# The first node stage of a two-layer graph kernel, rearranged

## The chip, the cores and the metric

One core of one Trainium2 chip runs the whole kernel. The metric is the device time of one launch in microseconds (us).

## The reference

There are 6250 nodes and 200000 edges, both with 128 features; the edges are sorted by target. Two layers follow each other, each as x = x + layer(relu(layernorm(x))).

```python
# layer 0, message passing
h = relu(layernorm(x))
msg = relu(concat([h[src], h[dst], edge_attr]) @ msg_W1 + msg_b1) @ msg_W2 + msg_b2
agg = segment_sum(msg, dst)
u   = relu(concat([h, agg]) @ upd_W1 + upd_b1) @ upd_W2 + upd_b2
x   = x + layer_norm(h + u, gamma, beta)
# layer 1, attention with 4 heads of 32, self loops added
h = relu(layernorm(x))
x_l, x_r = h @ W_l.T + b_l, h @ W_r.T + b_r
e = einsum(leaky_relu(x_l[src] + x_r[dst], 0.2), att)
alpha = segment_softmax(e, dst)
x   = x + elu(segment_sum(alpha * x_l[src], dst) + bias)
```

## The kernel before

Nodes are worked on in tiles of 128 (49 tiles, `NT`), edges in groups of 512 (391 groups, `J` = 4 edges per partition). A group's targets all lie in a window of 32 nodes (`W`) whose first row is `base[g]`, so target rows are read as a window and source rows are gathered.

The program has three parts. The first node stage (`prelude`, L347 and on) normalises all nodes, multiplies them by the first third of `msg_W1` and stores the product as the table `tab_a`; it also turns the edge indices into the layout that the edges need, checks that the windows hold (`flag_i`) and stores the first `LEAD` = 5 tiles of the target table `tab_b3` in three bf16 parts. Then comes the MLP edge stage, which also does all node work between the layers, and then the attention edge stage. If the check fails, a general path runs in place of both (`is_fast`, `If`/`Else` in every engine).

In each edge stage GpSimd issues four indirect gathers per group (L858), of 128 rows each, into a ring of eight slots. Its first gather comes after the last store of `tab_a` (`k.a_stored`), the stores of the zero rows at the tables' ends (`s_tops`) and the flag have arrived. SyncE loads the edge features, target rows and windows.

The first node stage goes in chunks of `CH` = 4 tiles, thirteen of them, the last with one tile. Each engine runs its own list of steps n in program order, tied to the others by semaphores:

- SyncE (`first_sync`) loads the nodes X in seven pieces cut at `XCUT`, the source and target rows (`row_loads`), 18 weights and biases, then stores one chunk of `tab_a` after the other (L471), with the remaining small loads and the eleven zero rows `tops` (L466) in between, and the permuted target rows `dst_rows` (L469).
- VectorE computes statistics of chunk n (L694, L697), and of chunk n-1 the reciprocal (L726) and the negative scaled mean `nm` (L727). In some steps it also makes constants (L701 to L712), copies turned index rows (`take_rows`, L683), prepares attention weights (L715 to L722), makes `base` and the window ids (L748 to L751) and counts edges inside their window (L753 to L760) and ordered bases (L762 to L774).
- ScalarE does the square root of chunk n (L517), the relu copy of turned chunk n-2 into `HT` (L521), the scaling of three tiles of chunk n-1 (L529), and copies the product of chunk n-3 to the store's buffer (L536), of which there are two, so it waits for the store of two chunks before.
- GpSimd scales the fourth tile (L580), casts both index tables to float (L588, L591) and permutes the target rows (L593).
- TensorE turns chunk n-1 (L627), multiplies chunk n-2 (L635), and in some steps turns index rows (L609) and spreads the bases over the partitions (L657).

After the stage SyncE loads the first eight groups' edges (`load_edges`), stores the early target tiles (`store_early`, L480), waits for both stores and loads the eight windows (`load_targets`).

Of the kernel before, what the change touches and what calls it, by code (L numbers as in the profile page):

```python
# [14 lines left out]
BF16 = mybir.dt.bfloat16  # L15
# [15 lines left out]
LEAD = 5  # L31
TINY = 1e-16
# [66 lines left out]
def gnn_program(nc, t):  # L99
# [22 lines left out]
    assert k.groups % U == U - 1 and CH < LEAD <= 2 * CH and NR - 1 <= NT  # L122
# [224 lines left out]
def prelude(nc, t, k, ctx, sems, ring, xn, at, r1, spare, stats):  # L347
# [7 lines left out]
    assert 2 * NBLK <= U and G * J <= 4 * EG  # L355
    s, s_x, s_ast, s_bst = k.first

    def sb(name, shape, dt=F32):
# [4 lines left out]
    rel = ring[:, 0:U].rearrange("p u j d -> p (u j d)")[:, 0:G * J].rearrange("p (g j) -> p g j", j=J)  # L363
    hit = ring[:, 0:U].rearrange("p u j d -> p (u j d)")[:, 4 * EG:4 * EG + G * J]
    perm = sb("perm", [GB, NBLK, EG], I16)
    cnt = sb("cnt", [P, 4])
    warm = sb("warm", [P, 1])
# [5 lines left out]
    b3 = [spare[:, 0:6 * P].bitcast(BF16).rearrange("p (t c d) -> p t c d", t=CH, c=3),  # L373
          spare[:, 6 * P:6 * P + (LEAD - CH) * 3 * P // 2].bitcast(BF16).rearrange("p (t c d) -> p t c d", c=3, d=P)]
# [63 lines left out]
    def first_sync(sp):  # L438
        sp.wait_ge(s["s_zt"], 1)
        for n, (a, b) in enumerate(zip(cuts, cuts[1:])):  # L440
            if n == 2:
                sp.wait_ge(s["s_pool"], 2)
                row_loads(sp, 0, "src", s["s_src"])
# [5 lines left out]
        if len(cuts) < 4:  # L449
            sp.wait_ge(s["s_pool"], 2)  # L450
            row_loads(sp, 0, "src", s["s_src"])
        row_loads(sp, 1, "dst", s["s_dst"])
        sp.wait_ge(s["s_pool"], 3)
        z16 = k.zrow[:].bitcast(BF16)[:, 0:P]
        top = k.NP - W
        tops = [(tab[top:k.NP, part, :], z16) for tab in (k.tab_b3, k.tab_r3) for part in range(3)]
        tops += [(tab[top:k.NP, :], k.zrow[:]) for tab in (k.tab_b, k.tab_r, k.tab_a, k.tab_l)]
        tops.append((k.tab_es[:, top:k.NP], k.zrow[0:H, 0:W]))
        for dst, src in weights[:8]:
            sp.dma_start(dst, src).then_inc(s["s_wt"], 16)  # L460
        for c in range(NC):
            for dst, src in weights[8 + 5 * (c - 1):8 + 5 * c if c < NC - 1 else None] if c else []:
                sp.dma_start(dst, src).then_inc(s["s_wt"], 16)
            if c == min(5, NC - 1):
                for dst, src in tops:
                    sp.dma_start(dst, src).then_inc(s["s_tops"], 16)  # L466
            if c == min(9, NC - 1):
                sp.wait_ge(s["s_conv"], 3)
                sp.dma_start(k.dst_rows.rearrange("(b g) e -> g b e", g=GB), perm[:]).then_inc(s["s_permout"], 16)  # L469
            sp.wait_ge(s["a_a"], c + 1)  # L470
            sp.dma_start(k.tab_a[c * CH * P:(c * CH + size(c)) * P, :].rearrange("(t p) d -> p t d", p=P),  # L471
                         at[c % 2][:, 0:size(c), :]).then_inc(s_ast[c % 2], 16)
        sp.wait_ge(s["s_permout"], 16)
# [3 lines left out]
    def store_early(sp):  # L477
        for c in range(2):
            sp.wait_ge(s["a_lo"], c + 1)
            sp.dma_start(k.tab_b3[c * CH * P:(c * CH + early(c)) * P, :, :].rearrange("(t p) c d -> p t c d", p=P),  # L480
                         b3[c][:, 0:early(c)]).then_inc(s_bst[c], 16)
        for one in s_bst:
            sp.wait_ge(one, 16)
# [26 lines left out]
    def first_scalar(act):  # L510
# [3 lines left out]
        for n in range(NC + 3):  # L514
# [8 lines left out]
            if 0 <= n - 1 < NC:  # L523
# [3 lines left out]
                for q in range(min(size(c), CH - 1)):  # L527
# [13 lines left out]
        for c in range(2):  # L541
# [6 lines left out]
    def first_gpsimd(pool):  # L548
# [26 lines left out]
        def scale(c):  # L575
            if size(c) == CH:
                i = c * CH + CH - 1
                pool.wait_ge(s["a_nm"], c + 1)
                after(pool, s["a_tp"], c - 1)
                pool.tensor_scalar(xn[c % 2][:, CH - 1, :], k.X[:, i, :], rs[:, i:i + 1], nm[:, i:i + 1], ALU.mult,  # L580
                                   ALU.add).then_inc(s["a_xp"], 1)

        for c in range(max(NC, NBLK + 4)):
            if c < NC:
                scale(c)
            if c == 0:
                pool.wait_ge(s["s_src"], n_rows)
                pool.tensor_copy(rows_f[:, 0], rows_i[:, 0]).then_inc(s["s_conv"], 1)  # L588
            if c == 3:
                pool.wait_ge(s["s_dst"], n_rows)  # L590
                pool.tensor_copy(rows_f[:, 1], rows_i[:, 1]).then_inc(s["s_conv"], 1)  # L591
            if 0 <= c - 4 < NBLK:
                last = pool.tensor_copy(perm[:, c - 4, :].rearrange("g (j p) -> g j p", j=J),  # L593
                                        rows_i[:, 1, c - 4, :].rearrange("g (p j) -> g j p", j=J))
                if c - 4 == NBLK - 1:
                    last.then_inc(s["s_conv"], 1)
# [5 lines left out]
    def first_tensor(pe):  # L602
# [10 lines left out]
        for n in range(steps):  # L613
            if n == 2:
                pe.wait_ge(s["s_w1"], 16)
            if n == 9:
# [27 lines left out]
            if n == 6:  # L644
                for b in range(min(2, NBLK)):
                    turn_rows(NBLK + b)
            if n == 7:
                for b in range(2, NBLK):
                    turn_rows(NBLK + b)
            if n == 11:  # L650
# [4 lines left out]
            if n == 9:  # L655
# [5 lines left out]
        pe.wait_ge(s["a_a"], NC)  # L661
        for c in range(2):
            for q in range(early(c)):
                i = c * CH + q
                last = pe.matmul(p_ab[c][:, q * P:(q + 1) * P], lhsT=k.HT[:, i * P:(i + 1) * P],
# [5 lines left out]
    def first_vector(dve):  # L671
# [18 lines left out]
        for n in range(steps):  # L690
# [8 lines left out]
            if n == 1:  # L699
# [13 lines left out]
            if n == 10:  # L713
# [9 lines left out]
            if 0 <= n - 1 < NC:  # L723
                c = n - 1
                dve.wait_ge(s["a_sd"], c + 1)
                link(dve.reciprocal(rs[:, tiles(c)], sd[:, tiles(c)]))  # L726
                dve.scalar_tensor_tensor(out=nm[:, tiles(c)], in0=mv[:, tiles(c), 0], scalar=-1.0, in1=rs[:, tiles(c)],  # L727
                                         op0=ALU.mult, op1=ALU.mult).then_inc(s["a_nm"], 1)
            if n == 4:
                for b in range(min(2, NBLK)):  # L730
                    take_rows(b)
            if n == 5:
                for b in range(2, NBLK):
                    take_rows(b)
            if n == 7:
                for b in range(min(2, NBLK)):
                    take_rows(NBLK + b)
            if n == 8:
                for b in range(2, NBLK):
                    take_rows(NBLK + b)  # L740
            if n == 13:
# [3 lines left out]
            if n == 10:  # L745
                dve.wait_ge(s["s_conv"], 3)
# [5 lines left out]
            if n == 11:  # L752
                link(dve.tensor_tensor(rel, k.dst_t[:, 0:G, :],  # L753
                                       k.base[:].unsqueeze(2).to_broadcast([P, G, J]), ALU.subtract))
            if n == 11:
                hits = hit.rearrange("p (g j) -> p g j", j=J)
# [21 lines left out]
        for c in range(2):  # L778
            dve.wait_ge(s["a_bp"], c + 1)
            dve.tensor_tensor(bt[c][:, 0:early(c), :],  # L780
                              p_ab[c][:, 0:early(c) * P].rearrange("p (t d) -> p t d", d=P),
                              k.b1_bc[:].unsqueeze(1).to_broadcast([P, early(c), P]), ALU.add).then_inc(s["a_b"], 1)
        for c in range(2):
# [3 lines left out]
        for c in range(2):  # L787
# [7 lines left out]
    return first_sync, store_early, first_scalar, first_gpsimd, first_tensor, first_vector  # L795
# [1608 lines left out]
```

## Time and profile before

| | us |
|---|---|
| median of 3 runs | 4030.74 (4029.25 to 4032.33) |
| the profiled execution | 4030.37 |
| its span, first to last instruction | 4028.5 |
| TensorE busy | 2958.8 (73%) |
| VectorE busy | 1939.5 (48%) |
| ScalarE busy | 1763.4 (44%) |
| GpSimd busy | 2986.6 (74%) |
| mean granted TensorE clock | 0.809 |

Busy time is a share of the whole span. GpSimd's busy time is nearly all gathers; the short time in which it issues each of them isn't counted as busy. A releaser that a view names is inferred from the semaphores.

### The profile page before, as it was taken

The page shows a single profiled execution, that of the slowest core. Times are in us where ns is not written, and L with a number is a line of the kernel's source. Part 1 is how long each engine was busy: PE and PEld are TensorE (multiplying, and loading weights), DVE is VectorE, ACT ScalarE, POOL GpSimd, SP SyncE. Part 2 cuts the span into 40 slices and gives each one's busy share as a digit, 9 for nine tenths or more (in the row PEclk, how much of TensorE's full clock was granted, in tenths as well). Part 3 has the DMA queues.
Part 4 walks back from the last instruction along what each step waited for, and adds up shares of the span by engine and source line. Part 5 has one row for each costly group of instructions (what it writes and reads, how often), then busy time and mean ns, then how long its engine had stood idle before and what let it go on. Part 6 is the DMA issues. An engine that isn't in the chain of part 4 may idle for free.

```text
span 4028.5 us, 83733 instructions
## 1 busy us (share of the span) xinstructions
PE 2958.8 (73%) x29662; PEld 2146.4 (53%) x29662; DVE 1939.5 (48%) x7746; ACT 1763.4 (44%) x4374; POOL 2986.6 (74%) x3167
## 2 busy tenths in 40 slices
PE   5877777778787787777867777766777766766776
PEld 4666666666666666666634444444444444444443
DVE  5334343444343434343435555555555555555555
ACT  4233333333333333333335555555555555555555
POOL 5777777777777777777757777777777777777775
PEclk8787787877787878787768888888888888888888
DMA  6444444444444444444423333333333333333332
GB/s 179 133 136 137 136 139 136 137 137 136 136 137 136 137 136 137 136 139 133 118 76 86 86 89 86 88 86 87 87 86 87 86 87 86 87 86 87 87 87 61
DMA packets 335748, 447.91 MB, mean 111 GB/s; under 512 B 150181, under 2 KB 190595, under 8 KB 335327
## 3 DMA queue, kind: packets, MB, share of 16 engines
q1 hardware_dynamic: 234831, 237.29, 19.9%
q0 software_dynamic: 100096, 205.00, 18.8%
q8 instruction: 241, 3.95, 0.4%
q14 instruction: 180, 1.47, 0.1%
q10 hardware_dynamic: 400, 0.20, 0.0%
HBM read 422.12 MB, written 20.07 MB: 110 GB/s over the span
## 4 chain that ended last, share of the span: by engine, by line
POOL 43%; PE 19%; DMA 17%; issue 17%; DVE 3%; ACT 2%; SPq 1%; DVEq 0%; POOLq 0%; ACTq 0%
POOL m_ring L858 27%; POOL t_ring L858 16%; DMA t_ring<-tab_l,src_t 13%; PE bank L2202 3%; DMA m_ring<-tab_a,src_t 3%; PE bank L2196 3%; PE bank L1473 3%; PE bank L2193 2%; PE bank L1465 1%; PE bank L2211 1%; PE bank L2214 1%; DVE m_pre L1560 1%; PE bank L2186 1%; PE bank L1475 1%; PE bank L1483 1%
## 5 line engine op out<-in xcount | busy, mean ns | idle before, releaser
L858 POOL DMA_INDIRECT t_ring<-tab_l,src_t x1564 | 1481.9, 948 | 500.7 <-issue 366.7
L858 POOL DMA_INDIRECT m_ring<-tab_a,src_t x1564 | 1484.9, 949 | 485.4 <-issue 468.3
L1560 DVE TENSOR_TENSOR m_pre<-bank,m_ring 128x512 f32<-128x512 f32 x391 | 270.3, 691 | 1109.5 <-DMA m_ring<-tab_a,src_t 813.9
L1521 ACT ACTIVATE m_hid<-m_pre 128x512 f32<-128x512 f32 x391 | 246.5, 631 | 1131.8 <-DVE m_pre L1560 1120.8
L1473 PE MATMUL bank<-w,m_attr_t 128*128 128x128 f32 x3128 | 703.1, 352 | 15.3 <-ACT m_attr_t L1517 15.3
L1473 PEld LDWEIGHTS bank<-w,m_attr_t 128*128 128x128 f32 x3128 | 608.7, 242 | 59.4 <-DVE m_hot L1551 23.8
L2193 PE MATMUL bank<-t_hot_t,t_win 96*128 96x512 bf16 x391 | 166.3, 425 | 571.0 <-DMA t_ring<-tab_l,src_t 498.8
L2242 ACT ACTIVATE t_z<-bank 128x512 f32<-128x512 f32 x391 | 233.4, 597 | 706.3 <-PE bank L2196 703.5
L2202 PE MATMUL bank<-t_zt,att_wn 128*128 128x512 f32 x782 | 537.8, 778 | 0.0
L2341 DVE TENSOR_TENSOR t_old<-acc,t_shrink 128x64 f32<-128x64 f32 x391 | 90.4, 231 | 804.1 <-ACT t_shrink L2253 674.9
L1475 PE MATMUL bank<-m_win,m_hot_t 96*128 96x128 bf16 x1564 | 393.5, 252 | 0.0
L2193 PEld LDWEIGHTS bank<-t_hot_t,t_win 96*128 96x128 bf16 x391 | 38.5, 98 | 657.7 <-issue 491.9
L2211 PEld LDWEIGHTS bank<-t_a_edge,t_ring 128*32 128x32 f32 x12512 | 157.9, 125 | 414.7 <-issue 406.1
L1483 PE MATMUL bank<-m_hid,m_hot 128*32 128x129 f32 x3128 | 188.7, 318 | 244.7 <-ACT m_hid L1521 243.9
L1465 PE MATMUL bank<-ident,m_ring 128*128 128x128 f32 x1564 | 303.9, 329 | 18.3 <-DMA m_win<-tab_b 18.3
L2237 ACT ACTIVATE t_a_edge<-bank 128x512 f32<-128x512 f32 x391 | 232.6, 595 | 193.3 <-PE bank L2186 188.0
L2196 PE MATMUL bank<-ident,t_ring 128*128 128x128 f32 x1564 | 286.2, 314 | 0.0
L1517 ACT ACTIVATE m_attr_t<-bank 128x512 f32<-128x512 f32 x391 | 229.8, 588 | 128.3 <-PE bank L1465 127.9
L2247 ACT ACTIVATE t_a_row<-t_logit,t_den_max 128x512 f32<-128x512 f32 x391 | 278.7, 713 | 0.5 <-DVE t_den_max L2309 0.5
L2256 ACT ACTIVATE t_pen<-t_hot_t,t_big 128x512 f32<-128x512 bf16 x391 | 277.5, 710 | 0.0
L2303 DVE TENSOR_TENSOR t_zt<-bank,t_z 128x512 f32<-128x512 f32 x391 | 264.0, 675 | 10.3 <-ACT t_z L2242 10.3
L2309 DVE CUSTOM_DVE_ANT_0 t_logit<-bank,t_pen 128x512 f32<-128x512 f32 x391 | 265.5, 679 | 1.1 <-PE bank L2202 1.0
(252 smaller groups left out, 5163.4 us busy)
## 6 DMA issues: line engine op xcount, KB each, us to landing
m_ring<-in_edge_attr_dram SPq DMA_DIRECT2D x390, 256.0 KB
t_rows<-dst_rows SPq DMA_DIRECT2D x196, 256.0 KB
m_rows<-dst_rows SPq DMA_DIRECT2D x196, 192.0 KB
m_ring<-tab_a,src_t POOLq DMA_INDIRECT x1564
t_ring<-tab_l,src_t POOLq DMA_INDIRECT x1564
m_win<-tab_b SPq DMA_DIRECT2D x391, 24.0 KB
t_win<-tab_r SPq DMA_DIRECT2D x391, 24.0 KB
tab_b<-n_b SPq DMA_DIRECT2D x47, 96.0 KB
```

The source lines that it names most:

```text
L858: pool.indirect_dma_start(out=r.got[u][0:rows, j, :], out_offset=None, in_=table, in_offset=bass.IndirectOffsetOnAxis(ap=k.src_t[0:rows, g ...
L1465: last = pe.transpose(p_attr[u % 2][:, j * P:(j + 1) * P], attr[u][:, j, :], k.ident[:])
L1473: pe.matmul(p_hid[q % 2][:, e], lhsT=attr_t[q % 2][:, e], rhs=k.w1[:, 2, :], start=True, stop=False)
L1475: last = pe.matmul(p_hid[q % 2][:, e], lhsT=hot_t[q % 2][0:3 * W, e], rhs=r.win[q][:], start=False, stop=True)
L1560: dve.tensor_tensor(pre[q % 2][:], p_hid[q % 2][:], r.got[q][:].rearrange("p j d -> p (j d)"), ALU.add).then_inc(s["m_sum"], 1)
L2193: pe.matmul(p_z[q % 2][:], lhsT=r.win[q][:], rhs=hot_t[q % 2][0:3 * W, :], start=True, stop=False)
L2196: last = pe.matmul(p_z[q % 2][:, j * P:(j + 1) * P], lhsT=r.got[q][:, j, :], rhs=k.ident[:], is_transpose=True, start=False, stop=(j == J ...
L2202: pe.matmul(p_e[q % 2][:], lhsT=k.att_wn[:], rhs=zt[q % 2][:], start=True, stop=True).then_inc(s["t_ep"], 1)
L2247: act.activation(a_row[q % 2][:], logit[q % 2][:], ACT.Exp, scale=-1.0, bias=den_max[q % 4][:, 1:2], accum_out=den_max[q % 4][:, 0:1]).the ...
L2256: act.activation(pen[q % 4][:], hot_t[q % 2][:], ACT.Identity, bias=big[:, 0:1], scale=-BIG).then_inc(s["t_pen"], 1)
L2303: dve.tensor_tensor(zt[q % 2][:], p_z[q % 2][:], z02[q % 2][:], ALU.max).then_inc(s["t_z"], 1)
L2309: dve.tensor_tensor_reduce(out=logit[q % 2][:], in0=p_e[q % 2][:], in1=pen[q % 4][:], scale=1.0, scalar=3.0e38, op0=ALU.add, op1=ALU.min, ...
```

## The change

All of it lies in the first node stage and in SyncE's first round after it.

- GpSimd scales two of a chunk's four tiles (`SCALED` = 2), ScalarE two.
- The check that every edge lies in its group's window is made on the index rows, which have 98 partitions with 4 x 512 entries (a group each): GpSimd clips each row to its window (`clip_rows`), and one VectorE pass counts the entries that clipping left as they were. The four passes over the turned layout of 1568 entries go.
- SyncE loads four pieces of nodes before the source and target rows, the rest after them, the last piece after the first table store. The 18 small loads and 11 zero rows are issued three at a time ahead of each table store. The permuted rows are stored after the twelfth chunk's store (before: before the tenth's).
- The casts, the turning of index rows, the base and the weight work come one to three steps later; VectorE's `reciprocal` and `nm` come ahead of the steps' extra work.
- The early target tiles are made and stored as two and three tiles (before: four and one), each finished before the next is begun; the first window is loaded between the two stores, and the edge loads of later groups come between the windows.

```diff
+SCALED = 2
+FRONT = 2
...
+    ends = sb("row_ends", [GB, 2, NBLK])
+    clipped = k.acc[0:GB, 0, P:P + NBLK * EG].rearrange("p (b e) -> p b e", b=NBLK)
...
     def early(c):
-        return min(CH, LEAD - c * CH)
+        return (LEAD - FRONT) if c else FRONT
...
     def first_sync(sp):
...
+        for n in range(min(4, many)):
+            load_nodes(n)
+        sp.wait_ge(s["s_pool"], 2)
+        row_loads(sp, 0, "src", s["s_src"])
+        row_loads(sp, 1, "dst", s["s_dst"])
+        for n in range(4, many - 1):
+            load_nodes(n)
+        store_sources(0)
+        if many > 4:
+            load_nodes(many - 1)
+        sp.wait_ge(s["s_pool"], 3)
+        small = [(dst, src, s["s_wt"]) for dst, src in weights] + [(dst, src, s["s_tops"]) for dst, src in tops]
+        per = -(-len(small) // max(min(10, NC - 2), 1))
+        for c in range(1, NC):
+            for dst, src, done in small[per * (c - 1):per * c if c < NC - 1 else None]:
+                sp.dma_start(dst, src).then_inc(done, 16)
+            store_sources(c)
+            if c == NC - 2:
+                sp.wait_ge(s["s_conv"], 3)
+                sp.dma_start(k.dst_rows.rearrange("(b g) e -> g b e", g=GB), perm[:]).then_inc(s["s_permout"], 16)
...
     def first_scalar(act):
-                for q in range(min(size(c), CH - 1)):
+                for q in range(CH - SCALED if size(c) == CH else size(c)):
...
     def first_gpsimd(pool):
+                for q in range(CH - SCALED, CH):
+                    i = c * CH + q
+                    last = pool.tensor_scalar(xn[c % 2][:, q, :], k.X[:, i, :], rs[:, i:i + 1], nm[:, i:i + 1],
+                                              ALU.mult, ALU.add)
+                last.then_inc(s["a_xp"], 1)
+        def clip_rows():
+            pool.tensor_scalar(ends[:, 0, :], rows_f[:, 1, :, 0], float(k.NP - W), 0.0, ALU.min, ALU.max
+                               ).then_inc(s["s_pool"], 1)
+            pool.wait_ge(s["s_pool"], 6)
+            pool.tensor_scalar(ends[:, 1, :], ends[:, 0, :], float(W - 1), None, ALU.add).then_inc(s["s_pool"], 1)
+            pool.wait_ge(s["s_pool"], 7)
+            for b in range(NBLK):
+                last = pool.tensor_scalar(clipped[:, b, :], rows_f[:, 1, b, :], ends[:, 0, b:b + 1],
+                                          ends[:, 1, b:b + 1], ALU.max, ALU.min)
+            last.then_inc(s["s_pool"], 1)
-            if c == 0:
+            if c == 2:     # cast of the source rows
-            if c == 3:
+            if c == 4:     # cast of the target rows
+            if c == 5:
+                pool.wait_ge(s["s_conv"], 2)
+                clip_rows()
-            if 0 <= c - 4 < NBLK:
+            if 0 <= c - 7 < NBLK:     # permutation
...
     def first_tensor(pe):
-            if n == 3:                # turn_rows: 3, 4, 6, 7
+            if n == 5:                # 5, 6, 7, 8
-            if n == 9:                # weights turned, base spread
+            if n == 11:               # weights turned
+            if n == 10:               # base spread
-        pe.wait_ge(s["a_a"], NC)
         for c in range(2):
+            pe.wait_ge(s["a_a"], NC - 1 + c)
...
     def first_vector(dve):
-            if n == 1:                # constants, ahead of reciprocal and nm
+            if n == 3:                # constants, behind them
-            if n == 10:               # weights, ahead of reciprocal and nm
+            if n == 12:               # weights, behind them
-            if n == 4:                # take_rows: 4, 5, 7, 8
+            if n == 7:                # 7, 8, 9, 10
-            if n == 10:               # base, window ids
+            if n == 11:
-            if n == 11:
-                link(dve.tensor_tensor(rel, k.dst_t[:, 0:G, :],
-                                       k.base[:].unsqueeze(2).to_broadcast([P, G, J]), ALU.subtract))
-                link(dve.tensor_scalar(hits, rel, 0.0, None, ALU.is_ge))
             if n == 12:
-                link(dve.scalar_tensor_tensor(out=rel, in0=rel, scalar=float(W), in1=hits, op0=ALU.is_lt, op1=ALU.mult))
-                link(dve.tensor_reduce(cnt[:, 0:1], rel, mybir.AxisListType.XY, ALU.add))
+                link(dve.memset(cnt[:], 0.0))
+                dve.wait_ge(s["s_pool"], 8)
+                link(dve.scalar_tensor_tensor(out=clipped, in0=clipped, scalar=0.0, in1=rows_f[:, 1], op0=ALU.add,
+                                              op1=ALU.is_equal, accum_out=cnt[0:GB, 0:1]))
...
         def fast_sync(sp):
-                    for u in slots:
+                    for u in range(2):
                         load_edges(sp, u, u)
-                    store_early(sp)
-                    for u in slots:
+                    store_early(sp, 0)
+                    early_stored(sp, 0)
+                    load_targets(sp, 0, 0)
+                    store_early(sp, 1)
+                    load_edges(sp, 2, 2)
+                    early_stored(sp, 1)
+                    for u in range(1, U):
                         load_targets(sp, u, u)
+                        if u + 2 < U:
+                            load_edges(sp, u + 2, u + 2)
```

The remarks behind `#` are put in here; they name the code that moves, unchanged, and its steps before and after.

## Rows read from the trace of the kernel before

**Rows 1.** The page's groups: line, engine, operation, count, busy us, mean ns, idle before.

```profile
L858 POOL DMA_INDIRECT m_ring<-tab_a,src_t x1564 | 1484.9, 949 | 485.4 <-issue 468.3
```

**Rows 2.** GpSimd's waits, whole span: total us, times, longest us.

```profile
POOL m_ring L858 <- issue: 468.3, 1508, 8.9
...
POOL t_ring L858 <- DMA tab_l<-m_attr_t: 24.3, 1, 24.3
...
POOL m_ring L858 <- PE bank L1475: 11.6, 38, 0.3
```

**Rows 3.** Timeline of GpSimd: start us, length us, what, idle before it.

```profile
60.62 1.26 POOL L858 DMA_INDIRECT m_ring<-tab_a,src_t  x1 [8.86 <-issue]
...
2021.16 0.90 POOL L858 DMA_INDIRECT m_ring<-tab_a,src_t  x1 [0.30 <-issue]
2046.37 0.95 POOL L858 DMA_INDIRECT t_ring<-tab_l,src_t  x1 [24.31 <-DMA tab_l<-m_attr_t]
```

**Rows 4.** Timeline of all engines, first 30 us.

```profile
6.81 0.15 DVE L701 TENSOR_SCALAR thirds<-thirds 128x42 f32<-128x42 f32 x1
...
9.24 1.26 ACT L529 ACTIVATE m_attr_t<-X,nm,rs 128x128 f32<-128x128 f32 x3 [2.02 <-DVE nm L727]
...
11.47 0.87 DVE L694 BATCH_NORM_STATS2 m_hid<-X 128x6 f32<-128x128 f32 x4 [2.26 <-DMA X<-in_x_dram]
...
17.65 0.60 ACT L536 ACTIVATE m_pre<-bank 128x512 f32<-128x512 f32 x1
...
23.32 1.89 POOL L591 CAST m_ring<-m_ring 98x2048 f32<-98x2048 int32 x1 [6.79 <-DMA m_ring<-in_dst_dram]
23.34 1.89 DVE L727 SCALAR_TENSOR_TENSOR nm<-mv,rs 128x4 f32<-128x4 f32 x1
...
27.73 0.45 POOL L580 TENSOR_SCALAR m_attr_t<-X,rs,nm 128x128 f32<-128x128 f32 x1 [0.91 <-DVE nm L727]
```

**Rows 5.** Timeline of all engines, 30 to 78 us.

```profile
31.04 0.60 ACT L536 ACTIVATE m_pre<-bank 128x512 f32<-128x512 f32 x1 [1.70 <-DMA tab_a<-m_pre]
...
37.82 0.30 ACT L517 ACTIVATE sd<-mv,eps 128x4 f32<-128x4 f32 x1 [1.13 <-DVE mv L697]
...
40.13 0.29 ACT L517 ACTIVATE sd<-mv,eps 128x4 f32<-128x4 f32 x1
...
43.02 0.57 DVE L748 TENSOR_SCALAR base<-bank 128x392 f32<-128x392 f32 x1 [2.07 <-PE bank L657]
...
53.50 0.16 DVE L727 SCALAR_TENSOR_TENSOR nm<-mv,rs 128x1 f32<-128x1 f32 x1
...
57.06 0.28 ACT L536 ACTIVATE m_pre<-bank 128x128 f32<-128x128 f32 x1 [0.95 <-DMA tab_a<-m_pre]
...
77.04 1.97 PE L1465 MATMUL bank<-ident,m_ring 128*128 128x128 f32 x8 [18.27 <-DMA m_win<-tab_b]
```

**Rows 6.** Groups by shape, GpSimd and VectorE, first stage.

```profile
L593 POOL CAST perm<-m_ring 98x512 int16<-98x512 int32 x4 | 4.4, 1104 | 0.0
...
L760 DVE TENSOR_REDUCE cnt<-m_ring 128x1 f32<-128x1568 f32 x1 | 1.8, 1786 | 0.0
L759 DVE SCALAR_TENSOR_TENSOR m_ring<-m_ring 128x1568 f32<-128x1568 f32 x1 | 1.8, 1785 | 0.0
L753 DVE TENSOR_TENSOR m_ring<-dst_t,base 128x1568 f32<-128x1568 f32 x1 | 1.8, 1782 | 0.0
L757 DVE TENSOR_SCALAR m_ring<-m_ring 128x1568 f32<-128x1568 f32 x1 | 1.1, 1116 | 0.0
```

**Rows 7.** Chain of waits in order of time: start us, us, what.

```profile
24.32 6.63 DMA tab_a<-m_pre
...
54.69 2.28 DMA tab_a<-m_pre
```

**Rows 8.** Stretches of 2 us: busy per engine, TensorE clock, DMA share, GB/s.

```profile
10.00:12.00 2.00, 1.09 (x4) 0.71 (x4) 0.53 (x3) 0.51 (x2) 1.84 (x1) 1.00 1.20 290
...
18.00:20.00 2.00, 2.00 (x11) 2.00 (x11) 0.00 (x0) 1.54 (x5) 0.00 (x0) 1.00 1.02 233
```

More of the change, by code:

```diff
@@ L121, in gnn_program @@
     k.ahead = min(k.NT - 1, NR)
-    assert k.groups % U == U - 1 and CH < LEAD <= 2 * CH and NR - 1 <= NT
+    assert k.groups % U == U - 1 and FRONT < LEAD <= FRONT + CH and LEAD * 3 <= 16 and NR - 1 <= NT
     assert k.tiles >= NR - 4 and NR > 4
@@ L354, in prelude @@
     cuts = [c for c in XCUT if c < NT] + [NT]
-    assert 2 * NBLK <= U and G * J <= 4 * EG
+    assert 2 * NBLK <= U and G <= EG
     s, s_x, s_ast, s_bst = k.first
@@ L438, in first_sync, with load_nodes @@
     def first_sync(sp):
[L439 to L443, printed above, removed]
+        top = k.NP - W
+        z16 = k.zrow[:].bitcast(BF16)[:, 0:P]
+        tops = [(tab[top:k.NP, part, :], z16) for tab in (k.tab_b3, k.tab_r3) for part in range(3)]
+        tops += [(tab[top:k.NP, :], k.zrow[:]) for tab in (k.tab_b, k.tab_r, k.tab_a, k.tab_l)]
+        tops.append((k.tab_es[:, top:k.NP], k.zrow[0:H, 0:W]))
+        def load_nodes(n):
+            a, b = cuts[n], cuts[n + 1]
             if min(b, nt) > a:
@@ L448, in first_sync, with store_sources @@
                 sp.dma_start(k.X[0:k.LAST, nt, :], t["x"][nt * P:k.N, :]).then_inc(s_x[n], 16)
[L449 to L469, printed above, removed]
+        def store_sources(c):
             sp.wait_ge(s["a_a"], c + 1)
@@ L472, in first_sync @@
                          at[c % 2][:, 0:size(c), :]).then_inc(s_ast[c % 2], 16)
+        sp.wait_ge(s["s_zt"], 1)
+        many = len(cuts) - 1
+        for n in range(min(4, many)):
[18 more added lines that the diff above has]
+                sp.dma_start(k.dst_rows.rearrange("(b g) e -> g b e", g=GB), perm[:]).then_inc(s["s_permout"], 16)
         sp.wait_ge(s["s_permout"], 16)
@@ L475, in first_sync, with store_early, early_stored @@
         sp.wait_ge(s["s_tcopy"], 2 * NBLK)
[L477 to L483, printed above, removed]
+    def store_early(sp, c):
+        sp.wait_ge(s["a_lo"], c + 1)
+        sp.dma_start(k.tab_b3[first(c) * P:(first(c) + early(c)) * P, :, :].rearrange("(t p) c d -> p t c d", p=P),
+                     b3[c][:, 0:early(c)]).then_inc(s_bst[c], 16)
+    def early_stored(sp, c):
+        sp.wait_ge(s_bst[c], 16)
     def general_rows_tensor(pe):
@@ L660, in first_tensor @@
         pe.matmul(p_misc[:, 0:1], lhsT=k.ones[:], rhs=cnt[:, 2:3], start=True, stop=True).then_inc(s["s_flagp"], 1)
-        pe.wait_ge(s["a_a"], NC)
         for c in range(2):
+            pe.wait_ge(s["a_a"], NC - 1 + c)
             for q in range(early(c)):
-                i = c * CH + q
-                last = pe.matmul(p_ab[c][:, q * P:(q + 1) * P], lhsT=k.HT[:, i * P:(i + 1) * P],
+                i = first(c) + q
+                last = pe.matmul(p_ab[(NC + c) % 2][:, q * P:(q + 1) * P], lhsT=k.HT[:, i * P:(i + 1) * P],
                                  rhs=k.w1[:, 1, :], start=True, stop=True)
@@ L780, in first_vector @@
             dve.tensor_tensor(bt[c][:, 0:early(c), :],
-                              p_ab[c][:, 0:early(c) * P].rearrange("p (t d) -> p t d", d=P),
+                              p_ab[(NC + c) % 2][:, 0:early(c) * P].rearrange("p (t d) -> p t d", d=P),
                               k.b1_bc[:].unsqueeze(1).to_broadcast([P, early(c), P]), ALU.add).then_inc(s["a_b"], 1)
-        for c in range(2):
             dve.wait_ge(s["a_hi"], c + 1)
```

61 lines of the change are left out of this document (26 added, 35 removed).

## The prediction

> **What bounds the kernel now.** I read the page first, then GpSimd's waits over the whole span, then its timeline at its two starts, then the timeline of the first 66 us with the chain of waits through it.
>
> The page's costliest groups are the gathers of L858: 1564 in each of the two edge stages, about 0.95 us each [rows 1]. GpSimd's waits show what is between them: 0.30 us of issue each time, longer only twice. Once is 8.9 us before the first gather, once 24.3 us between the stages, where it waits for the stored table tab_l. A row that names TensorE as releaser has no wait over 0.3 us [rows 2], so no other engine holds the stream up. The first gather starts at 60.62, the last of the MLP stage ends at 2022.06, the next stage starts at 2046.37 [rows 3]. That is 1961.4 us for 1564 gathers, 1.254 us each, with nothing in it that this change touches. So the change is worth what it moves the first gather, one for one: time = 4030.37 - (60.62 - new start). The profiled execution's own 4030.37 is its span of 4028.5 plus 1.9 around it; the median of the runs is 4030.74, so I add 0.4 at the end.
>
> The reader should then look at what ends last before 60.62. I number as the code does: chunk c is 4 node tiles (12 chunks, and a 13th of one tile), at(c) is ScalarE's copy of its table rows (L536), nm(c) VectorE's L727, step n ScalarE's turn that begins with the square root of chunk n. GpSimd waits for the last tab_a store, which follows at(12) at 57.06, which follows nm(12) at 53.50 [rows 5]. From nm(12) to the first gather are 7.1 us.
>
> **The change part by part.** I follow four checkpoints: at(0), at(3), the start of step 10, nm(12). Before they are 17.65, 31.04, 40.13 and 53.50 [rows 4, 5].
>
> *Start.* The constants (L701 to L712) stood between the square root and nm(0), from 6.81 until ScalarE's scaling at 9.24 could start; they now come two steps later, which frees 2.0 us. It isn't this that decides: statistics of chunk 2 waited for their node load until 11.47 [rows 4], and 0.8 MB of source rows were ahead of it in the queue. At some 0.27 MB/us (0.29 in one stretch of the loads, 0.23 in a later one [rows 8]) these are 2.9 us, so chunk 2 arrives at about 8.6. From there at(0) came 6.2 us later; two scalings in this stretch now have two tiles on ScalarE, not three. One tile is 1.26/3 = 0.42 us [rows 4], so at(0) lands at 8.6 + 6.2 - 0.8 = 14.0, 3.6 earlier.
>
> *Stretch to at(3): transfers.* at(3) waited 1.70 us for the store of chunk 1, which the chain shows under way for 6.63 us behind weight loads [rows 5, 7]. By rates alone, the computing would now be at at(3) around 23. But the queue has a floor: ahead of the landing of that store stand the first weight (0.19 MB), all nodes (3.2), both row tables (1.6), the store of chunk 0 (0.26), three weights (0.26) and the store itself (0.26), 5.8 MB in all, since the last node load is now put between the stores of chunks 0 and 1. From 2 us on at 0.29 for nodes and 0.245 for rows that is 23.0, and 1.3 us until the store counts (2.28 us for one alone [rows 7], less its 0.95 us of bytes). So at(3) is at 24.4, 6.6 earlier. At 0.25 throughout it would be 26.4; with no queue at all, 23. The wait for destination rows (GpSimd idle 6.79 us until 23.32 [rows 4]) goes, since they land near 16; VectorE's nm(4), which was caught for 1.89 us behind that cast, is freed with it.
>
> *GpSimd's load in the middle.* It gets a second scaling per chunk: 0.45 us alone [rows 4], so 12 x 0.45 = 5.4 us in all, beside ScalarE's 0.84 of the same chunk and ready earlier, since it needn't wait for ScalarE's relu copy. Cost nothing while GpSimd is not late. The range check adds two short instructions (0.3 each at most) and four of 98x512. No row has this operation at this size. Below: 0.45 + 384 x 0.92 ns (the slope of the 98x2048 cast, 1.89 us [rows 4]) = 0.8 us. Above: four times the 128-wide one, 1.8. I take 1.1, the 98x512 cast of L593 [rows 6]. Check: 5.0 us (3.8 to 7.8). It starts after the destination cast and the scaling of chunk 5, near 19.3, so chunk 6 is scaled by 25.2; ScalarE's own half of chunk 6 isn't done before 26.6 (24.4, its own 0.6, root and relu copy 0.8, two tiles 0.84), as it is held by the store. Cover 1.4 us: nothing at 1.1 each, 1.4 us at 1.8. The Trainium skill, GPSIMD Engine Reference, section 3.1, gives 1.8 cycles per element for such a loop, 0.77 us for 512 elements. By it the check would be 3.7 us and as hidden; the sum stays.
>
> *at(3) to step 10.* This took 9.1 us [rows 5]. Three scalings lose a tile each (-1.3). The turning of rows is moved, but both pairs of destination rows lie in this stretch before and after. SyncE now issues three small loads before each store instead of eleven table tops in a block: stores of chunks 3 to 5 have two or three broadcasts ahead of them. The 6.63 us store had five, and exceeded a lone one by 4.3, mostly bytes; I allow 1.0 for these (0 to 3). So 9.1 - 1.3 + 1.0 = 8.8, step 10 starts at 33.2.
>
> *Step 10 to nm(12).* The base matmul is moved one step, so is VectorE's wait for it. Base (L748) started 5.2 us after the start of step 9 [rows 5]; now it is one tile less after that of step 10: +4.8. From there nm(12) was 10.5 us away. Four passes of 1568 elements go: 1.79 + 1.78 + 1.78 + 1.12 = 6.5 [rows 6]. One pass over 2048 comes: 1.785 x 2048/1568 = 2.3 (2.0 to 3.0; its accumulator is not in any row). Statistics of chunk 11 now precede base (-1.3), the weight block (1.4) moves behind it. 10.5 - 6.5 + 2.3 - 1.3 + 1.4 = 6.4; with memset and links 6.6. nm(12) = 33.2 + 4.8 + 6.6 = 44.6, 8.9 earlier.
>
> *nm(12) to the gather.* 7.1 us as before, with the same wait of at(12) for the store of chunk 10. New is that the permuted rows (392 x 1 KB) are stored between the last two table stores, not three chunks earlier: 0.4 MB is 1.5 us in the same queue, partly beside at(12). I take 1.0 (0 to 1.5). The flag is ready earlier: nine short operations follow nm(12), as before. First gather: 44.6 + 7.1 + 1.0 = 52.7, a shift of 7.9.
>
> *Target rows.* Storing two tiles first brings group 0's window long before the 77 us at which TensorE began [rows 5]; its eight groups of lead belong to the ring, and GpSimd didn't wait for TensorE even so [rows 2]. Worth nothing, costs nothing: the new chain of alternate VectorE and ScalarE work is longer, yet TensorE still starts some 15 us earlier.
>
> Sum: 4030.37 - 7.9 + 0.4 = 4022.8.
>
> **The rivals.**
> 1. *Stalls between the checkpoints eat part of it* (shift 2 to 6, say 4026.8). For it: queue at 0.25 (+2), GpSimd's check at the upper end (+1.4), the broadcasts at 3 (+2). All are bounds named above. Against: each has some cover.
> 2. *The middle runs freely* (shift 10 to 13, say 4019.3): TensorE is kept busy from earlier on, transfers land at 0.29 throughout and no store is waited for. For it: ScalarE's own work is only about 1.9 us a chunk. Against: the queue floor.
> 3. *Slower: GpSimd becomes the bound of the first stage.* VectorE's nm(4) took 1.89 us because GpSimd was casting [rows 4]; its two-input operations wait for GpSimd's current one. So a slow check on GpSimd, at chunk 5, holds both nm(6) and the scaling of chunk 6. It decides from 1.45 us an instruction (cover gone), and eats the whole gain from 1.45 + 7.9/4 = 3.4 us each; at 5.6 us each the kernel is 8.8 us slower, 4039. Against: nearest rows end at 1.8. The Trainium skill, GPSIMD Engine Reference, section 8, says that it shares its SBUF interfaces with VectorE and contends with two-input instructions; the row agrees (1.89 instead of 0.16), and it advises VectorE for elementwise work.
> 4. *It doesn't do what it says*: the new count differs from the constant that the flag compares with, and the general path runs, many times slower. The sentinel in padded rows is clipped to another value, so padding isn't counted, as before.
>
> **How the numbers follow.** 0.2% of 4030.7 is 8.1 us, about what a measurement here can tell from no change; my shift of 7.9 lies on it. Forecast (shift 6 to 10) 0.58, rival 1 0.19, rival 2 0.19, rival 3 0.03, rival 4 0.01. Over 8.1: half of the forecast's and all of rival 2's, 0.48. Within: 0.48. Slower: 0.04. Range: from a shift of 3 to one of 13, 4017.7 to 4027.8.
>
> **What would show it.** First gather between 51 and 55, gathers still 0.30 apart, the gap between stages still about 24 us. at(0) near 14, at(3) near 24 with a wait for a store, step 10 near 33, nm(12) near 45 with one pass of about 2.3 us ahead of it. GpSimd's four check instructions near 1.1 each. TensorE's edge work starting near 60 with nothing gained from it. The prediction is wrong if the first gather isn't the shift, or if ScalarE waits for GpSimd's half of chunk 6.

## The result and the profile after

| | before | after |
|---|---|---|
| median, same chip, 6 runs each | 4031.26 (4028.79 to 4034.16) | 4051.11 (4047.47 to 4051.82) |
| the profiled execution, and its span | 4030.37, 4028.5 | 4051.45, 4049.6 |
| first gather starts | 60.62 | 58.72 |
| one gather, median of 1564 and 1564 | 944 and 944 ns | 952 and 952 ns |
| mean granted TensorE clock | 0.809 | 0.811 |

The ratio is 1.0048 (1.0035 to 1.0061, a 95% interval): slower by half a per cent, where I had forecast 4022.8. Two things differ from the forecast. The first gather came 1.9 us earlier, not 7.9. And each gather takes longer, in both edge stages. From the page of the changed kernel, the rows that answer to [rows 1] (busy us, mean ns of one):

```profile
L880 POOL DMA_INDIRECT t_ring<-tab_l,src_t x1564 | 1493.1, 955 | 500.6 <-issue 368.4
L880 POOL DMA_INDIRECT m_ring<-tab_a,src_t x1564 | 1496.9, 957 | 487.8 <-issue 472.6
```

Before, the second of them was

```profile
L858 POOL DMA_INDIRECT t_ring<-tab_l,src_t x1564 | 1481.9, 948 | 500.7 <-issue 366.7
```

From 1484.9 and 1481.9 the busy time rose to 1496.9 and 1493.1, together 23.2 us. Less the 1.9 us of the earlier start that is 21.3; the spans differ by 21.1. Nothing else is left to explain. GpSimd's waits show that it isn't idleness, the answer to [rows 2] (us in total, times, longest):

```profile
POOL m_ring L880 <- issue: 472.6, 1514, 11.4
POOL t_ring L880 <- PE bank L2224: 56.7, 186, 0.3
POOL t_ring L880 <- DMA tab_l<-m_attr_t: 24.3, 1, 24.3
```

Still 0.3 us between gathers and 24.3 between the stages. So the instruction itself is slower. One view of the line of the gathers gives the median (min/median/max ns, first and last start); before and after:

```profile
L858 POOL DMA_INDIRECT m_ring<-tab_a,src_t x1564: 892/944/1257, 60.6 to 2021.2; - x196
L858 POOL DMA_INDIRECT t_ring<-tab_l,src_t x1564: 896/944/1083, 2046.4 to 4003.8; - x196
L880 POOL DMA_INDIRECT m_ring<-tab_a,src_t x1564: 896/952/1347, 58.7 to 2031.1; - x196
L880 POOL DMA_INDIRECT t_ring<-tab_l,src_t x1564: 897/952/1092, 2056.3 to 4024.9; - x196
```

The change doesn't touch these instructions: in both traces GpSimd issues the same 3128 gathers, in the same order, with the same shapes.

The first stage, from the timeline (start, length, line, operation, idle time before and what ended it), in place of [rows 4, 5]:

```profile
14.08 0.60 ACT L550 ACTIVATE m_pre<-bank 128x512 f32<-128x512 f32 x1 [0.34 <-PE bank L664]
14.50 1.89 POOL L614 CAST m_ring<-m_ring 98x2048 f32<-98x2048 int32 x1 [2.32 <-DMA m_ring<-in_src_dram]
14.63 1.77 DVE L732 SCALAR_TENSOR_TENSOR nm<-mv,rs 128x4 f32<-128x4 f32 x1
22.38 8.25 POOL L605 TENSOR_SCALAR acc<-m_ring,row_ends 98x512 f32<-98x512 f32 x4
24.84 0.60 ACT L550 ACTIVATE m_pre<-bank 128x512 f32<-128x512 f32 x1 [1.48 <-DMA tab_a<-m_pre]
25.86 0.16 DVE L732 SCALAR_TENSOR_TENSOR nm<-mv,rs 128x4 f32<-128x4 f32 x1
30.62 1.72 POOL L594 TENSOR_SCALAR m_attr_t<-X,rs,nm 128x128 f32<-128x128 f32 x4
31.59 1.08 PE L656 MATMUL bank<-ident,m_attr_t 128*128 128x128 f32 x4 [5.68 <-issue]
32.71 0.60 ACT L535 ACTIVATE HT<-bank 128x512 f32<-128x512 f32 x1 [5.17 <-PE bank L656]
38.34 0.29 ACT L531 ACTIVATE sd<-mv,eps 128x4 f32<-128x4 f32 x1
43.77 0.56 DVE L776 TENSOR_SCALAR base<-bank 128x392 f32<-128x392 f32 x1 [2.97 <-PE bank L686]
47.59 2.29 DVE L783 SCALAR_TENSOR_TENSOR acc<-acc,m_ring 98x2048 f32<-98x2048 f32 x1
50.12 0.16 DVE L732 SCALAR_TENSOR_TENSOR nm<-mv,rs 128x1 f32<-128x1 f32 x1
58.72 1.35 POOL L880 DMA_INDIRECT m_ring<-tab_a,src_t  x1 [11.43 <-issue]
```

| checkpoint | predicted | after | difference that arose since the last checkpoint |
|---|---|---|---|
| at(0) | 14.0 | 14.08 | +0.1 |
| at(3) | 24.4 | 24.84 | +0.4 |
| start of step 10 | 33.2 | 38.34 | +4.7, most of it the clipping on GpSimd (e8) |
| nm(12) | 44.6 | 50.12 | +0.4 |
| first gather | 52.7 | 58.72 | +0.5 |

The four clipping instructions (max with one end, min with the other) take 8.25 us, 2.06 each. They are in front of GpSimd's half of chunk 6 (30.62); TensorE stands still for 5.68 us until it can turn that chunk, and ScalarE's relu copy waits 5.17 us. VectorE isn't held by them: in the middle of the clipping `nm` takes 0.16 us (25.86). It was held by a cast on GpSimd, once more: nm(3) takes 1.77 us (14.63) beside the cast of the source rows (14.50).

TensorE's first work of the edge stage starts at 67.87, where it was 77.04; I had said near 60. The gathers don't wait for it.

### The profile page after: what moved, and what is told of

It is laid out like the page before. It is cut to its first block, busy times and chain, and to the rows that moved or that the text cites. A ratio compares the mean times of both kernels' runs of the same rounds, so it can differ in the third digit from the quotient of the medians.

```text
span 4049.6 us, 83736 instructions
## 1 busy us (share of the span) xinstructions
PE 2949.8 (73%) x29662; PEld 2139.6 (53%) x29662; DVE 1934.3 (48%) x7745; ACT 1759.2 (43%) x4362; POOL 3020.9 (75%) x3185
## 4 chain that ended last, share of the span: by engine, by line
POOL 45%; issue 18%; DMA 17%; PE 17%; DVE 2%; ACT 2%; SPq 0%; DVEq 0%; POOLq 0%; ACTq 0%
POOL m_ring L880 28%; POOL t_ring L880 17%; DMA t_ring<-tab_l,src_t 13%; DMA m_ring<-tab_a,src_t 3%; PE bank L2224 3%; PE bank L2230 3%; PE bank L1501 3%; PE bank L2221 2%; PE bank L1493 1%; DVE m_pre L1588 1%; PE bank L2239 1%; PE bank L2242 1%; PE bank L1503 1%; PE bank L1511 1%; PE bank L1518 0%
## 5 line engine op out<-in xcount | busy, mean ns | idle before, releaser
L880 POOL DMA_INDIRECT t_ring<-tab_l,src_t x1564 | 1493.1, 955 | 500.6 <-issue 368.4
L880 POOL DMA_INDIRECT m_ring<-tab_a,src_t x1564 | 1496.9, 957 | 487.8 <-issue 472.6
L2214 PE MATMUL bank<-ident,t_a_row 128*128 128x128 f32 x1564 | 267.8, 299 | 1.1 <-ACT t_a_row L2275 1.1
```

The source lines that it names most:

```text
L880: pool.indirect_dma_start(out=r.got[u][0:rows, j, :], out_offset=None, in_=table, in_offset=bass.IndirectOffsetOnAxis(ap=k.src_t[0:rows, g ...
L2214: last = pe.transpose(p_turn[:, e], a_row[q % 2][:, e], k.ident[:])
```

## The experiments

One theory is needed for each of the two losses. For the late first gather: *the clipping on GpSimd is slow and ScalarE and TensorE wait behind it.* For the slower gathers, where the trace shows no cause, the candidates were: I, that max/min ran on GpSimd at all; II, that GpSimd scales two tiles; III, the memory and the layout of the changed stage; IV, GpSimd's instruction count ahead of the gathers, or which instruction is last; V, the order of its clipping and its permutation of target rows (the last permutation is a cast to int16 at chunk 10, before at chunk 7). The recorded expectations name theories by letters of their own, each explained where it first comes.

The first four kernels and the last two (e13, e15) ran at a lower granted clock (0.70 to 0.72), where the kernel before takes 4933.56 and 4970.75 us and gathers do wait for other engines. Their totals (e1 4929.27, e2 4939.88, e3 4938.34, e4 4914.42, e13 4968.83, one execution each) can't be compared with the other ones, and so don't test the times that were expected of them. A gather's length can be compared: 944 ns (e1, e2) and 952 ns (e4, e13, e15) both come at this clock, as both come at 0.81.

**e1: clipping on VectorE at step 12.** The two short and four long instructions are moved from GpSimd to VectorE, otherwise after.

```diff
-            if c == 5:
-                pool.wait_ge(s["s_conv"], 2)
-                clip_rows()
...
             if n == 12:
+                for b in range(NBLK):
+                    last = dve.tensor_scalar(clipped[:, b, :], rows_f[:, 1, b, :], ends[:, 0, b:b + 1],
+                                             ends[:, 1, b:b + 1], ALU.max, ALU.min)
```

> The changed kernel, with the six clipping operations moved from GpSimd to VectorE (step 12). The traces of before and after show two things: the first gather starts at 58.7 instead of 60.6, and each of the 3128 gathers takes 952 instead of 944 ns (medians), 3128 x 7.5 ns = 23.5 us. Theory A (an operation of new kind on GpSimd, the clipping by max and min, leaves each later gather 8 ns slower): the gathers are back at 944 here. Theory B (the number of GpSimd's instructions or their place in the program sets it): 944 or 952, no link with clipping. In both, the stall in the middle (TensorE waited 5.7 us for chunk 6) goes, and VectorE gets about 2 us more: first gather at 53 to 56. So the time is about 4024 to 4026 by A, and 4047 by B if the gathers stay slow.

Measured: gathers 944 and 944 ns, first gather 57.00 (53 to 56 expected). The slower gathers hang on the clipping being on GpSimd; candidates II and III fall, since this kernel has both.

```profile
L871 POOL DMA_INDIRECT m_ring<-tab_a,src_t x1564: 894/944/1152, 57.0 to 2447.5; - x196
```

**e2: before, and clipping on GpSimd at chunk 9.** Its result is unused. In the kernel before, chunk 9 is behind the last permutation.

> The kernel before, with the same six clipping operations added on GpSimd behind its permutation; their result is used by nothing. Theory A: gathers at 952 ns, 4030 + 24 = 4054 plus a few us of stall. Theory B: gathers at 944 if nothing else moves them, time 4031 to 4036.

Measured: 944 and 944 ns, first gather 64.57. The same six instructions on the same engine, and no effect: candidate I falls as it stands, and with e1 the place of these six instructions is what is left to test.

**e3 and e4: the scaling alone.** e3 is before with two tiles scaled by GpSimd; e4 is after with `SCALED = 1`.

> The kernel before, with two tiles of a chunk scaled by GpSimd instead of one, nothing else changed. Theory A: gathers stay at 944 ns; the first gather starts 1 to 4 us earlier, 4027 to 4030. Theory B (number of GpSimd's instructions): 12 more instructions may move the gathers to 952, then about 4052.

> The changed kernel with one tile of a chunk scaled by GpSimd, as before, and the clipping left on it. Theory A: gathers stay at 952 ns, time 4050 to 4056. Theory B: 12 instructions fewer, gathers may be back at 944, then 4028 to 4032.

Measured: e3 947 and 946 ns, first gather 60.48, 0.1 us earlier than before and not 1 to 4; e4 952 and 952 ns, 58.60. Two scaled tiles aren't the cause of the 8 ns. The 2 to 3 ns of e3 stay unexplained.

**e5 and e6: the same clipping, late in after and early in before.** In e5 it comes at chunk 9 of after, still ahead of the last permutation; in e6 at chunk 5 of before, ahead of the last permutation too.

```diff
-            if c == 5:
+            if c == 9:
                 pool.wait_ge(s["s_conv"], 2)
                 clip_rows()
```

> The changed kernel with GpSimd's six clipping operations moved from its chunk 5 to its chunk 9. What is known: the gathers' instructions are the same in all kernels, yet their median is 944 ns in the kernel before, 952 in the changed one, 944 with the clipping off GpSimd, 944 with it added late to the kernel before, 952 in the changed kernel with one tile scaled, 946 to 947 with two tiles scaled in the kernel before. Theory C (the order of GpSimd's operations ahead of the gathers sets the gathers' time; clipping early gives 952): 944 here. Theory D (something of the changed kernel other than the place of clipping, together with clipping): 952. Either way TensorE's wait for chunk 6 goes, another for chunk 10 comes; first gather at 57 to 61.

> The kernel before with the six clipping operations added on GpSimd at its chunk 5, result unused. Theory C: gathers at 952 ns. Theory D: 944, as when they were added at chunk 9.

Measured: e5 952 and 952 ns, first gather 58.11, 4048.57 us; e6 952 and 952 ns, 67.95, 4062.15 us, where before took 4031.16. Nothing of the change but the clipping is in e6, and the gathers are slow:

```profile
L875 POOL DMA_INDIRECT m_ring<-tab_a,src_t x1564: 896/952/1196, 67.9 to 2041.7; - x196
```

and of e2, the same instructions behind the last permutation:

```profile
L875 POOL DMA_INDIRECT m_ring<-tab_a,src_t x1564: 896/944/1196, 64.6 to 2455.6; - x196
```

**e7: one memset as GpSimd's last operation.** After, and `pool.memset(ends[:, 0, 0:1], 0.0)` ahead of its waits for the stores.

> The changed kernel with one more GpSimd instruction, a memset of one column, as its last before it waits for the table stores. Theory E (the number of GpSimd's instructions ahead of the gathers, that is their place in its program, sets the time): another median than 952. Theories C and D: 952. First gather at 58.7 as in the changed kernel.

Measured: 952 and 952 ns, first gather 58.48, 4050.75 us. Candidate IV falls for this instruction: neither one more nor another last one helps. e2 and e6 have equally many instructions ahead of the gathers, and differ by 8 ns.

**e8: the whole row check in VectorE's gap.** Clipping and count go to VectorE at step 11, ahead of its wait for the bases, where it is idle; nothing of them is left on GpSimd.

```diff
             if n == 11:
+                for b in range(NBLK):
+                    last = dve.tensor_scalar(clipped[:, b, :], rows_f[:, 1, b, :], ends[:, 0, b:b + 1],
+                                             ends[:, 1, b:b + 1], ALU.max, ALU.min)
+                link(last)
+                link(dve.memset(cnt[:], 0.0))
+                link(dve.scalar_tensor_tensor(out=clipped, in0=clipped, scalar=0.0, in1=rows_f[:, 1], op0=ALU.add,
+                                              op1=ALU.is_equal, accum_out=cnt[0:GB, 0:1]))
                 dve.wait_ge(s["s_basep"], 1)
```

> The changed kernel with the clipping on VectorE and, with the counting pass, put ahead of VectorE's wait for the bases (step 11), where the trace of after has it idle for 2.97 us. Six clipping operations of 98x512 at most are about 2 us and the count 2.3 us. The stall of 5.2 us on GpSimd's half of chunk 6 goes and 2.3 us of counting leave the end: first gather at 52 to 55 instead of 58.7. With gathers at 944 ns (clipping not on GpSimd, as in the first such run) the time is 4022 to 4025 where before has 4031; with 952 it is 4046 to 4049.

Measured: 4025.18 us (4022.39 to 4026.87) against 4031.16, ratio 0.9983 (0.9974 to 0.9993). It is 0.2% faster than before, and 26 us under the 4051.11 of the changed kernel, though the two weren't timed side by side. From its timeline, and the view of its gathers:

```profile
33.71 0.29 ACT L531 ACTIVATE sd<-mv,eps 128x4 f32<-128x4 f32 x1
34.74 2.73 DVE L764 TENSOR_SCALAR acc<-m_ring,row_ends 98x512 f32<-98x512 f32 x4
37.63 2.29 DVE L768 SCALAR_TENSOR_TENSOR acc<-acc,m_ring 98x2048 f32<-98x2048 f32 x1
39.96 0.57 DVE L771 TENSOR_SCALAR base<-bank 128x392 f32<-128x392 f32 x1
43.83 0.16 DVE L718 SCALAR_TENSOR_TENSOR nm<-mv,rs 128x1 f32<-128x1 f32 x1
53.22 1.15 POOL L870 DMA_INDIRECT m_ring<-tab_a,src_t  x1 [9.74 <-issue]
```

```profile
L870 POOL DMA_INDIRECT m_ring<-tab_a,src_t x1564: 898/944/1152, 53.2 to 2014.1; - x196
L870 POOL DMA_INDIRECT t_ring<-tab_l,src_t x1564: 895/944/1077, 2039.4 to 3996.4; - x196
```

This is near the predicted stage: step 10 at 33.71 (33.2 predicted), nm(12) at 43.83 (44.6), the first gather at 53.22 (52.7). It isn't the same stage, since the count now stands ahead of the base: from step 10 to nm(12) are 10.1 us where 11.4 were predicted, from there to the gather 9.4 where 8.1 were. So the last number agrees in part by luck. VectorE does the four instructions in 2.73 us where GpSimd took 8.25. From at(3), which is at 24.23 here, to step 10 are 9.5 us, where after took 13.5: that is what the clipping on GpSimd cost there, 4.0 us. Against after, the span is 29.3 us shorter (4049.6 to 4020.3): 5.5 of it by the first gather, and nearly all of the rest, 23.8, by the gathers' busy time, 2967.1 for 2990.0 us, 7.3 ns each.

**e9 and e12: the order alone.** e9 is after with the clipping behind the last permutation (chunk 11). e12 is e6, early clipping, with one more 98x512 clipping instruction at chunk 9, behind it.

```diff
+            if c == NBLK + 7:
+                pool.wait_ge(s["s_conv"], 2)
+                clip_rows()
```

> The changed kernel with GpSimd's clipping moved behind its last permutation (chunk 11). So far the gathers' median was 952 ns where clipping ran before the last permutation (changed kernel at chunk 5 and 9, kernel before at chunk 5), 944 where it ran behind it (kernel before at chunk 9) or not on GpSimd. Theory F (what counts is whether the clipping or the permutation ran last): 944 ns. Theory D (the rest of the changed kernel with clipping on GpSimd anywhere): 952. The count now waits for the clipping: first gather at 63 to 67. Time by F 4036 to 4040, by D 4060 to 4064.

> The kernel before with the six clipping operations at chunk 5, as in the run that had 952 ns, and one more clipping of 98x512 at chunk 9, behind the last permutation. Theory F: 944 ns again, since a clipping runs last. Otherwise 952 ns. First gather near 68.

Measured: e9 946 and 946 ns, first gather 63.46, 4040.53 us; e12 944 and 944 ns, 66.65, 4036.42 us; before 4037.39 (one execution of each). Candidate V holds, though not as two levels: e9 was to have 944 ns by it and has 946. e12 differs from e6 by one more instruction, 2.06 us of added work, and the median gather is 8 ns shorter, the span 4034.5 instead of 4060.3:

```profile
47.10 2.06 POOL L610 TENSOR_SCALAR acc<-m_ring,row_ends 98x512 f32<-98x512 f32 x1
```

```profile
L879 POOL DMA_INDIRECT m_ring<-tab_a,src_t x1564: 896/944/1199, 66.7 to 2028.7; - x196
```

and of e9:

```profile
L880 POOL DMA_INDIRECT m_ring<-tab_a,src_t x1564: 897/946/1196, 63.5 to 2028.2; - x196
```

**e10, e11 and e13: the kind and the length of the operation.** Each is e8 with unused instructions on GpSimd at chunk 5. e10 has four 98x512 mult/add, e11 one 98x512 max/min, e13 one max/min of four columns. The scalars are two constants held per partition.

```diff
+            if c == 5:
+                pool.wait_ge(s["s_conv"], 2)
+                for b in range(1):
+                    pool.tensor_scalar(spare_rows[:, b, :], rows_f[:, 1, b, :], k.pm[0:GB, 0:1],
+                                       k.p3[0:GB, 0:1], ALU.max, ALU.min)
```

> The kernel with the whole check in VectorE's gap (first gather 53.2, gathers 944 ns), plus four GpSimd operations of 98x512 at chunk 5, in the clipping's place and shape, that multiply and add as the scaling does; result unused. Theory G (the kind, max and min, matters for the gathers): 944 ns. Theory H (any such work ahead of the permutation matters): 952. For the stage: if each takes 2.06 us as a clipping does, the length goes with the columns whatever the operation (0.44 us for 128, so 4.2 ns for each further column), and TensorE's wait of 5 us for chunk 6 is back; by my earlier 1.1 us each it would not be.

> As the last, with one GpSimd operation of 98x512 by max and min in place of four that multiply and add; result unused. Theory G: gathers at 952 ns after a single one. Theory H with dose: 944 to 947. The operation takes 2.06 us, chunk 6 is late by less than 1 us, first gather 53 to 54.

> e8 with one max/min of 98x4 instead of 98x512 on GpSimd at chunk 5, result unused. If the kind and the place of one instruction set the gathers' time and not its length: 952 ns per gather, first gather near 53.2, span near 4042. If it takes a long instruction: 944 ns and a span near 4020.

Measured: e10 944 and 944 ns; e11 952 and 952 ns, e13 952 and 952 ns. The added instructions, and the gathers, of e10:

```profile
21.08 3.01 POOL L611 TENSOR_SCALAR acc<-m_ring,pm,p 98x512 f32<-98x512 f32 x4
56.30 1.50 POOL L876 DMA_INDIRECT m_ring<-tab_a,src_t  x1 [11.49 <-issue]
```

```profile
L876 POOL DMA_INDIRECT m_ring<-tab_a,src_t x1564: 896/944/1497, 56.3 to 2019.8; - x196
```

of e11:

```profile
20.90 2.07 POOL L611 TENSOR_SCALAR acc<-m_ring,pm,p 98x512 f32<-98x512 f32 x1
53.24 1.17 POOL L876 DMA_INDIRECT m_ring<-tab_a,src_t  x1 [9.74 <-issue]
```

```profile
L876 POOL DMA_INDIRECT m_ring<-tab_a,src_t x1564: 892/952/1172, 53.2 to 2024.0; - x196
L876 POOL DMA_INDIRECT t_ring<-tab_l,src_t x1564: 896/952/1090, 2049.1 to 4018.1; - x196
```

and of e13:

```profile
20.35 0.38 POOL L611 TENSOR_SCALAR acc<-m_ring,pm,p 98x4 f32<-98x4 f32 x1
```

```profile
L876 POOL DMA_INDIRECT m_ring<-tab_a,src_t x1564: 896/952/1208, 54.8 to 2454.9; - x196
```

e8 and e11 are the cleanest pair (though on two chips, one execution each, and executions of one kernel differ by up to 6 us here): the first gathers start at 53.22 and 53.24, the last ones at 3996.4 and 4018.1. One instruction of 2.07 us, which doesn't delay the first gather, comes with 21.7 us over the 4 ms behind it, and the gathers' busy time accounts for all of it: 2988.8 for 2967.1 us, 6.9 ns each. e10 and e11 ran on one chip: from the first gather to the last are 3945.3 and 3964.9 us, 19.6 apart, and the gathers' busy time differs by 19.8. By e13 it takes only an instruction of 0.38 us: length doesn't matter, kind does. e10 differs from e8 in another way: base and nm(12) came 1.3 us and the first gather 3.1 us later. How much of that its 3.01 us on GpSimd made isn't separated from the change of chip. Its one execution took 4027.72, where e11's took 4043.97 on the same chip.

**e15: e11 timed in rounds.** The same kernel.

> The same kernel as e11 (e8 and one unused 98x512 max/min on GpSimd), timed. If its 21.6 us over e8 are the gathers' and repeat: 1.0030 to 1.0035 times the kernel before, 4043 to 4045, slower by more than the measurement's uncertainty. If e11's time was one of that execution alone: 0.998, as e8.

Measured: 4962.78 against 4970.75, ratio 0.9988 (0.9976 to 0.9999). The expected 1.0030 didn't come; the ratio is that of the other case named, in which e11's time would have been one of that execution alone. The trace gives another reading, which isn't tested by a timed run: its gathers take 952 ns here as well, but at this clock they often wait for others, as rows of its gathers' view show (waited for, us, times; `remote` is a releaser that the view doesn't resolve):

```profile
  remote: 701.1, 450
  DVE acc L1593: 258.0, 119
```

In e11, where the granted clock is 0.81, no gather waits for `remote`, and the second row is 1.2 us in 4 times. So the price of 8 ns per gather was seen in the total only where gathers are back to back. There it rests on the timed before and after (+20 us with a first gather 1.9 earlier), on the timed e8 (-6 against before, 7.4 earlier), and on the single executions of e5 (+17, 2.5 earlier), e6 (+31, 7.3 later) and e11.

## Why the prediction was wrong

**The step that failed.** "That is 1961.4 us for 1564 gathers, 1.254 us each, with nothing in it that this change touches. So the change is worth what it moves the first gather, one for one". The first sentence's numbers were right, and the edge stages' instructions aren't touched. But a gather's own 944 ns isn't a constant of the instruction: with a max/min ahead of the last permutation it is 952 ns. Over 3128 gathers that is 23.2 us of busy time (7.4 ns each by the mean), twelve times the 1.9 us that the stage still gained. I had a rival for stalls between checkpoints, for a floor in the queue, for a slow first stage, and none for slower gathers; the slower case had 0.04 for that reason.

**The second step, of the sum.** "I take 1.1, the 98x512 cast of L593", with 1.8 as the upper bound: 2.06 measured. The two rows were a cast and a mult/add, and kind decides: on 98x512, mult/add takes 0.75 us (e10: 3.01 for four), the cast 1.1, max/min 2.06 (e11: 2.07). By the 0.38 us at four columns (e13) and the 2.07 at 512, a max/min column is some 3.3 ns. The Trainium skill, GPSIMD Engine Reference, section 3.1, gives 0.77 us for 512 elements as the best case: mult/add agrees, max/min is 2.7 times that. "Cost nothing", resting on a cover of 1.4 us, was wrong by a stall of 5.68 us on TensorE. This is rival 3 at 2.06 us. Its price there, 4 x (2.06 - 1.45) = 2.4 us, was too small, since the clipping began at 22.38, not near 19.3: from at(3) to step 10 it cost 4.0 us (13.5 for the 9.5 of e8). Nor did it work through VectorE, as rival 3 had it ("holds both nm(6) and the scaling of chunk 6"): `nm` took 0.16 us beside the clipping, and 1.77 beside a cast. With the check taken off GpSimd and out of the end of VectorE's chain (e8) the first gather comes 5.5 us earlier, at 53.22. So this second step took 4 to 5 of the forecast's 7.9 us and alone would have left a gain of 1.9; the first step made it a loss.

**What held.** The start and the queue: at(0) 14.08 for 14.0, at(3) 24.84 for 24.4, with the wait for a store (1.48) that I gave it. The count in one pass: 2.29 us for 2.3. From base to nm(12) 6.35 us for 6.6. From nm(12) to the first gather 8.60 us for 8.1. The gap of 24.3 us between the stages and the 0.30 us between gathers. Storing two target tiles first brought TensorE's edge work forward by 9.2 us, not by the 15 or so that I gave it, and moved no gather. A stage without clipping on GpSimd gives 4025.18, inside the range of 4017.7 to 4027.8: in e8, a different kernel, a gather keeps its length and the first one's shift sets the time, as the forecast had it. For the kernel as changed that was wrong.

**What stays open.** Which mechanism in GpSimd makes a gather 8 ns longer. The runs show what the 952 ns follow: kind (a max/min, not four mult/add), order (ahead of the last permutation cast, without another max/min behind it), not the length of the instruction. This fits something that GpSimd keeps between instructions, such as where its routines stand in its memory, but no view shows that, and it is argued only. The 946 to 947 ns of e3 and e9 fit no two-level account, and e3 has no max/min on GpSimd at all. That another operation behind the last permutation (a mult/add tensor_scalar) would also restore 944 wasn't tried as such; the scalings of the last chunks, which are mult/add, follow it in after without restoring it.

## What to carry to other kernels

Where thousands of like instructions run back to back on one engine, compare the median length of one before and after, first of all: 8 ns times 3128 is more than any stall of the first stage. Take a duration for an operation from a row of the same operation; another kind on the same tile differed by 2.7 times. Elementwise work that GpSimd does beside a chain of alternate engines belongs where an engine is idle anyway: the same row check took 8.25 us of GpSimd and 2.29 of VectorE in after, and 5.0 us of VectorE (2.73 + 2.29) in e8.

## What the runs showed of the hardware

- On GpSimd a max/min tensor_scalar with pointer scalars of 98x512 takes 2.06 us, a mult/add one 0.75; on VectorE the max/min takes 0.68 (2.73 for four).
- An indirect gather of 128 rows on GpSimd has a median of 944 or 952 ns (946 to 947 in e3 and e9) in both edge stages of a launch, by what GpSimd ran 20 to 40 us before the first of them (e12: 47.10 to 66.65; e6: 28.26 to 67.95), even if it is one instruction of four columns (e13).
- VectorE's `nm`, which reads two tensors, took 1.77 us beside a cast of 98x2048 on GpSimd and 0.16 us beside its max/min (after).
- In the runs with a granted clock of 0.70 to 0.72 for 0.81 the gathers' length is the same (944 and 952 ns), and the kernel before takes 4933.56 to 4970.75 us for 4031; gathers then wait for other engines, and 20 us of GpSimd didn't show in the total (e15).
